# Two attention layers, experts and a recurrent cell in one pipelined kernel: the gate's weights on GpSimd, output products two a round, other orders of the instructions

## What is computed

```
layer 0: x = x + attention(norm(x), ctx)     16 heads of 8, with biases
         x = x + experts(norm(x))            gate scores over 8 experts, the best 2 count,
                                             weighted by their scores; relu between W1 and W2
layer 1: x = x + attention(norm(x), ctx)     no biases
         x = x + cell(norm(x))

cell(x): c = sigmoid(x wf + c uf + bf) * c + sigmoid(x wi + c ui + bi) * tanh(x wc + c uc)
         over the steps t; then tanh(x_t wo + c_final uo + bo) for every t
```

## Time and profile of the kernel before

| what | value |
|---|---|
| profiled execution, device time | 869.94 us |
| span from its first to its last instruction | 868.2 us |
| median of the three runs | 869.86 us |
| mean granted TensorE clock | 0.991 |
| busy: TensorE, VectorE, ScalarE, GpSimd | 836.5, 789.6, 782.3, 624.0 us |

### The profile page before, as it was taken

The page is one execution under the profiler, slowest core; times in us unless marked ns, Lnnn a source line. Parts: engine busy times, 40 slices in busy tenths (PEclk is TensorE's granted clock), DMA queues, the critical chain, the costliest instruction groups (busy, mean ns, idle before and its releaser), DMA issues. The chain is left out here.

```text
span 868.2 us, 41445 instructions
## 1 busy us (share of the span) xinstructions
PE 836.5 (96%) x15262; PEld 745.8 (86%) x15262; DVE 789.6 (91%) x2965; ACT 782.3 (90%) x2488; POOL 624.0 (72%) x1098
## 2 busy tenths in 40 slices
PE   5699999999999999999999999999999999999887
PEld 3488899999999999999999999999999999898765
DVE  4789999999999999999999999999999999999834
ACT  4699999999999999999999999999999999888754
POOL 4777887777877787777777777778777877766514
PEclk9999999999999999999999999999999999999999
DMA  9400000000000000000000000000000000000005
GB/s 337 165 3 2 3 3 4 3 4 3 3 3 3 3 3 4 3 3 4 3 4 3 3 4 3 3 4 3 4 3 3 3 3 4 3 4 2 3 2 194
DMA packets 6822, 17.68 MB, mean 20 GB/s; under 512 B 736, under 2 KB 2016, under 8 KB 6624
## 3 DMA queue, kind: packets, MB, share of 16 engines
q1 hardware_dynamic: 6336, 14.50, 4.4%
q10 hardware_dynamic: 288, 0.53, 0.2%
HBM read 10.84 MB, written 4.19 MB: 17 GB/s over the span
## 5 line engine op out<-in xcount | busy, mean ns | idle before, releaser
L1072 POOL TENSOR_TENSOR h<-Ex 128x512 f32<-128x512 f32 (+1 forms) x144 | 165.9, 1152 | 43.0 <-ACT Ex L613 42.4
L806 DVE TENSOR_REDUCE mx<-ps 128x8 f32<-128x512 f32 (+1 forms) x288 | 173.4, 623 | 14.5 <-PE ps L308 13.7
L820 DVE TENSOR_TENSOR Ex<-ps,mx 128x512 f32<-128x512 f32 (+1 forms) x288 | 172.7, 620 | 0.0
L323 PE MATMUL ps<-w,Ex 128*128 128x128 f32 x1024 | 164.0, 278 | 4.4 <-DVE Ex L820 2.9
L624 ACT ACTIVATE ET<-ps 128x512 f32<-128x512 f32 (+1 forms) x288 | 163.4, 567 | 1.2 <-PE ps L323 0.9
L613 ACT ACTIVATE Ex<-Ex 128x512 f32<-128x512 f32 (+1 forms) x288 | 164.4, 597 | 0.0
L1056 POOL TENSOR_TENSOR rs<-ve,half 128x4 f32<-128x4 f32 (+3 forms) x77 | 70.4, 914 | 128.5 <-DVE ve L796 125.8
L930 DVE SCALAR_TENSOR_TENSOR acc<-ps,we,acc 128x128 f32<-128x128 f32 x448 | 151.8, 339 | 6.0 <-PE ps L409 3.4
L662 ACT ACTIVATE hT<-ps,w 128x128 f32<-128x128 f32 x512 | 147.1, 382 | 3.4 <-PE ps L388 2.9
L388 PEld LDWEIGHTS ps<-xT,w 128*128 128x128 f32 x1024 | 124.2, 191 | 24.6 <-issue 24.6
L409 PE MATMUL ps<-w,hT 128*128 128x128 f32 x1024 | 141.8, 281 | 1.1 <-DVE Ex L820 1.0
(11 more groups left out here) (105 smaller groups left out, 1800.3 us busy)
## 6 DMA issues: line engine op xcount, KB each, us to landing
out_dram<-x SPq DMA_DIRECT2D x15, 256.0 KB, 2.7
cx<-ctx_dram SPq DMA_DIRECT2D x7, 512.0 KB, 12.7
x<-x_dram SPq DMA_DIRECT2D x7, 512.0 KB, 13.6
w<-weights_dram SPq DMA_DIRECT2D x2, 576.0 KB, 7.6
w<-weights_dram SPq DMA_DIRECT2D x1, 512.0 KB, 5.4
w<-weights_dram ACTq DMA_DIRECT2D x1, 264.0 KB, 3.7
w<-weights_dram ACTq DMA_DIRECT2D x1, 256.0 KB, 3.2
cx<-ctx_dram SPq DMA_DIRECT2D x1, 256.0 KB, 5.5
```

The costliest lines, as they stand in the source:

```text
L323: m = e.transpose(b[:, 128 * n:128 * n + 128], Ex[:, j % 2, r, 128 * n:128 * n + 128], ident)
L806: e.tensor_reduce(mx[:, j % 2, r, 4 * lo:4 * hi], b[:, 256 * lo:256 * hi].rearrange("p (j k) -> p j k", k=64), AX.X, ALU.max).then_inc(sig ...
L820: e.tensor_tensor(Ex[:, j % 2, r, 256 * lo:256 * hi].rearrange("p (j k) -> p j k", k=64), b[:, 256 * lo:256 * hi].rearrange("p (j k) -> p ...
L1072: e.tensor_tensor(u, v[:, :, :, 0:32], v[:, :, :, 32:64], ALU.add).then_inc(sig("half1"), 1)
```

## The change

1. **Gate's weights on GpSimd.** `gate_float` and `gate_weights` of VectorE are gone. GpSimd's `gate_sum` now does the conversion and the two products as well, each with a wait for the one before.
2. **Output products.** `NW` goes from 8 to 9 groups, in two uses `wx0` and `wx1` a round, from round 72 on; the first five `inputs_share` groups follow them in the same places, so all fourteen are made in rounds 72 to 78. Behind the loop come the biases, `uo` and the `cell_share` of each group. The banks of the tail are named anew (`ENDS`), since the last transposes still hold one. VectorE adds cU's part for four groups of two tiles instead of one, `TAIL` has 18 groups.
3. **First keys.** The keys of tile 0 are made in round 0 instead of 1; those of the others stay.
4. **Biases and clearing in parts.** The eight steps of `bias_pieces` run two a round in rounds 1 to 4; b2 moves from the file of W2 to that of Wq, which is loaded earlier. The clearing runs in four parts in rounds 6 to 9. `project_bias` and its sum run a round later.
5. **Orders.** All engines' lists, `LAG` and `USES` (23 uses) are new. Some parts move a round: xT is copied at lag 1 instead of 0, qT at 1 instead of 2, e0, e3 and the sums at 4 instead of 3, y1 and the first four additions at 3 instead of 2. In the new list the seventh before `pv` is S0, before `q` S1, before `yb` S2, before `wx1` S3. L1, L2, L3 stay, and so does the round of the last half step; `LAST` is one less.
6. **Warm-up.** VectorE clears `acc` at the start, and TensorE makes five products of 128 x 128 by 256 columns of these zeros before it waits for the identity.

```diff
+NW, EARLY = 9, 5
+WARM = 5
-WIDTHS = [512, 161, 528, 1024, 1152, 256, 1152]
+WIDTHS = [512, 161, 656, 1024, 1024, 256, 1152]
...
             def keys_values(i):
                 t = i - LAG["kv"]
-                if not on(t):
+                if t == 0 or not -1 <= t < NT:
                     return
                 b = bank(i, "kv")
+                t = max(t, 0)
...
+            def out_inputs(i, u):
+                g = 2 * (i - LAST_STEP + 6) + u
+                if not 0 <= g < NW + EARLY:
+                    return
+                if g >= NW:
+                    inputs_share(g - NW)
+                    return
...
+            e.wait_ge(sig("zeros"), 1)
+            for n in range(WARM):
+                e.matmul(lstm[:, 0:256], acc[:, 0, :], acc[:, :, :], start=True, stop=True)
...
+                turn_e(i, 0)
+                experts(i, 1)
                 step(i, 1)
+                turn_e(i, 3)
                 gate(i)
-                turn_e(i, 2)
                 turn_w(i)
                 turn_r(i)
-                out_inputs(i)
+                turn_e(i, 2)
                 hidden(i, 0)
-                turn_e(i, 1)
+                out_inputs(i, 0)
                 scores(i)
                 hidden(i, 1)
                 cell_inputs(i)
-                expert_bias(i)
+                turn_e(i, 1)
                 keys_values(i)
                 step(i, 0)
                 values(i)
+                query(i)
+                expert_bias(i)
+                out_inputs(i, 1)
                 experts(i, 0)
-                turn_e(i, 3)
                 turn_x(i)
-                turn_e(i, 0)
-                experts(i, 1)
                 project(i)
-                query(i)
...
+                exps(i, 1)
+                exps(i, 0)
+                out_inputs(i, 1)
+                turn_x(i)
+                widen(i)
                 turn_e(i, 0)
-                widen(i)
                 gates(i, 1)
-                query(i)
+                turn_w(i)
+                turn_e(i, 3)
+                turn_r(i)
                 turn_e(i, 2)
...
                 scale(i)
                 gates(i, 0)
                 keys_values(i)
-                exps(i, 0)
-                exps(i, 1)
-                turn_e(i, 3)
-                turn_x(i)
+                query(i)
...
-                if i == FIRST + 6:
-                    bias_pieces()
+                if FIRST + 1 <= i < FIRST + 5:
+                    bias_pieces(2 * (i - FIRST) - 2)
+                    bias_pieces(2 * (i - FIRST) - 1)
...
-                e.wait_ge(sig("wab"), t + 1)
+                e.wait_ge(sig("tix"), t + 1)
+                e.tensor_copy(tif[:, s, :], tix[:, s, 0:2]).then_inc(sig("tif"), 1)
+                e.wait_ge(sig("tif"), t + 1)
+                e.tensor_scalar(wa[:, s, :], iota, tif[:, s, 0:1], top[:, s, 0:1], ALU.is_equal, ALU.mult)
+                e.tensor_scalar(wb[:, s, :], iota, tif[:, s, 1:2], top[:, s, 1:2], ALU.is_equal,
+                                ALU.mult).then_inc(sig("wab"), 1)
...
+                gate_pieces(i)
+                spread_values(i)
+                add_bias(i)
                 keys(i, 1)
                 halves(i, 0)
-                spread_values(i)
                 spread(i)
                 gate_sum(i)
                 halves(i, 1)
                 keys(i, 0)
-                add_bias(i)
-                gate_pieces(i)
```

More of the change, by code:

```diff
@@ L112, in build @@
         identb = sb("identb", [P, 128], BF16)
-        half = sb("half", [P, 4])
         xn = sb("xn", [P, 2, 4, 128])
@@ L116, in build @@
         mv = sb("mv", [P, 2, 4, 2])
+        half = sb("half", [P, 4])
         ones = sb("ones", [P, 8])
+        nm = sb("nm", [P, 2, 4])
         ve = sb("ve", [P, 2, 4])
-        nm = sb("nm", [P, 2, 4])
         mr = sb("mr", [P, 2, 4])
@@ L185, in bank_of, with end_bank @@
             return banks[(len(USES) * (j + LAG["S" if name[0] == "S" else name]) + PLACE[name]) % 7]
+        last = bank_of("turnx", NT + L3 - 1)
+        ENDS = [b for b in banks[0:7] if b is not last] + [last, lstm]
+        def end_bank(k):
+            return ENDS[MINE.index(k) % EARLY] if k in MINE else ENDS[5 + 2 * (SIDE.index(k) % 2)]
         def sync_program(e):
@@ L433, in out_inputs, with inputs_share, cell_share @@
                                  skip_group_check=True)
-                m.then_inc(sig("wx"), 1)
+                m.then_inc(sig(f"wx{u}"), 1)
+            def inputs_share(m):
+                lo = TAIL[MINE[m]][1]
+                if m == 0:
+                    for name, reader, _, chain, step, first in USES:
+                        if name != "turnx":
+                            e.wait_ge(sig(reader), step * (SPAN[chain][1] - 1) + first)
+                if m >= EARLY:
+                    e.wait_ge(sig("out"), MINE[m - EARLY] + 1)
+                e.wait_ge(sig("xT"), lo + 4 + L3)
+                for n in range(4):
+                    e.matmul(end_bank(MINE[m])[:, 128 * n:128 * n + 128], cx[:, lo + n, :], wT[:, WX, :], start=(n == 0),
+                             stop=False, skip_group_check=True)
+            def cell_share(m):
+                e.matmul(end_bank(MINE[m])[:, :].rearrange("p (t d) -> p t d", t=4), ident,
+                         cU[:, :].unsqueeze(1).to_broadcast([P, 4, 128]), start=False, stop=True,
+                         skip_group_check=True).then_inc(sig("pre_pe"), 1)
             def cell_inputs(i):
@@ L498, in tensor_program @@
                 values(i)
+                query(i)
+                expert_bias(i)
+                out_inputs(i, 1)
                 experts(i, 0)
-                turn_e(i, 3)
                 turn_x(i)
-                turn_e(i, 0)
-                experts(i, 1)
                 project(i)
-                query(i)
-            for _, reader, _, chain, step, first in USES:
-                e.wait_ge(sig(reader), step * (SPAN[chain][1] - 1) + first)
-            for n in (6, 5):
-                e.matmul(banks[n][:, 0:128], ident, bo1, start=True, stop=False, skip_group_check=True)
-            inputs_share(0)
+            for n in (5, 6):
+                e.matmul(ENDS[n][:, 0:128], ident, bo1, start=True, stop=False, skip_group_check=True)
             e.wait_ge(sig("C"), 2 * NT + 1)
@@ L515, in tensor_program @@
                 for g in (0, 64):
-                    m = e.matmul(banks[n][g:g + 64, 0:128], c_end, wT[:, UO, :], start=False, stop=True,
+                    m = e.matmul(ENDS[n][g:g + 64, 0:128], c_end, wT[:, UO, :], start=False, stop=True,
                                  skip_group_check=True)
                 m.then_inc(sig("uo"), 1)
-            for m in range(1, 5):
-                inputs_share(m)
             e.wait_ge(sig("cU"), 1)
-            for m in range(len(mine)):
-                if m >= 5:
+            for m in range(len(MINE)):
+                if m >= EARLY:
                     inputs_share(m)
@@ L978, in vector_program @@
                 combine(i, 8)
[L979 removed]
+                stats_inputs(i)
+                update(i, 1)
                 stats_experts(i)
```

195 lines of the change are left out of this document (81 added, 114 removed), and 30 rows, old and new, of tables (LAG, USES).

## The result

The changed kernel takes 853.17 us (median of 4 runs, 852.65 to 853.61) against 868.69 us (4 runs, 866.58 to 869.94): ratio 0.9826, interval 0.9806 to 0.9847. The forecast was 851.5 us, range 845 to 861. The profiled execution took 852.91 us, its span is 851.1, against 869.94 and 868.2: 17.1 us of span.

A forecast was written before the change was run, and what follows sets the result against it. TensorE was taken to bound the full rounds, leaving gains at the two ends. Filling with start -11.5, idling up to 130 us -0.5, drain +1.0 and tail -7.4 gave -18.4 us: 851.5 us, range 845 to 861.

The forecast's parts named there:

- The tail: From the last half step to the end: 7.4 us won, with cU and the outputs coming sooner.
- the 0.3 us for a last half step at full clock: In the tail: 0.3 us more won if the last half step takes 0.54 us instead of 0.87.
- Bias pieces: In parts in rounds 1 to 4, they end TensorE's 3.68 us idling in round 5, which goes from 9.77 to 5.5 us.
- The start: Up to the first scores: they begin 1.5 us sooner, at 10.0 us instead of 11.47.
- The filling rounds: Rounds 2 to 6, up to the scores of round 7: 10 us won beyond the start's 1.5 us.
- The path to the next scores becomes that of the keys: Filling rounds: scores, key products, copy and Km set the round, 4.9 us each in rounds 2 and 3.
- the rival that I gave 0.13 for rounds 4 to 6: Half clock in the filling: each of these rounds some 1.3 us longer, 855.5 us in all; chance 0.13.
- full clock from the start: Rival: the products on zeros raise the clock, scores at 9.3 us, rounds 2 and 3 at 3.9, 849 us; chance 0.10.
- Full rounds: The 49 rounds from 130.38 to 732.84 us: no change, within 3 us either way.
- The drain: Rounds 72 to 78: 1.0 us lost to the added output groups in rounds 72 and 73, bounds 0 and 1.8.
- the rival to which I gave 0.08: Drain: each of six added groups lengthens its round by 0.9 us, 5.4 less the 1.0 counted, 856 us; chance 0.08.
- The slower case: A stall in every full round, TensorE waiting for ScalarE's late rT; with 0.45 us a round 873.5 us; chance 0.07.

The follow-up runs named there:

- shares_behind: Changed kernel with the five early output groups of rounds 76 to 78 made behind the last half step; ratio 0.9895 to the kernel before.
- before_parts: Kernel before with only the bias pieces in parts (b2 in the file of Wq) and the clearing in four parts; 861.93 us against 868.40, ratio 0.9922.
- bias_block: Changed kernel with all eight bias pieces together ahead of round 6 and the clearing in one; ratio 0.9884 to the kernel before.
- keep_clock: Changed kernel with six more products on zeros in rounds 3 to 5 and the output bias product a round later; ratio 0.9824 to the kernel before.
- no_warm: Changed kernel without the five warm-up products on zeros; ratio 0.9859 to the kernel before.
- exps_later: Changed kernel with two of ScalarE's exponentials, in rounds before 7, moved behind its later copies; ratio 0.9872 to the kernel before.
- gate_behind_step: Changed kernel with the gate's product directly behind the half step, ahead of the transposes; ratio 0.9867 to the kernel before.
- drain_moved: Changed kernel with four early groups and the nine product groups in rounds 70 to 76, a second one in 74 and 75; ratio 0.9811 to the kernel before.

## Why the prediction was right, and where it was not

**The tail** (7.4 forecast, 6.9 measured) was right step by step: cU at 3.4 us, the first cell share at 3.7, VectorE's list without a gap (9.91 us for 18 groups), DMA engines full, end at 18.7 us. One term was counted twice: the 0.3 us for a last half step at full clock was added to steps that had that half step at full clock already (they count 0.5 us of it). shares_behind shows that the groups made early carry the gain. What was not foreseen is the clock: without them it fell, in this order of the instructions, and the tail lost 1.4 us more than their own length. Likewise before_parts won 1.4 us in its tail without touching it, by its clock alone. Of the 6.9 us won, then, some 1.4 may be the clock's, an estimate from these two traces.

**Bias pieces** were the surest part of the filling: 3.7 us of idling and the half clock behind it, in both directions (bias_block +4.3 us at round 7, before_parts -5.3). Both kernels move the clearing along with the pieces, so what it gives by itself is not shown. The parts ran cheaply in rounds 1 and 2 (both subtractions 0.289 us). The last two, in round 4, met Km. The instructions of VectorE's line 961 in the changed kernel (shortest, median and longest in ns, starts in us), and then GpSimd's timeline at that place:

```profile
L961 DVE SCALAR_TENSOR_TENSOR b2s<-b2p,w,b2s x2: 339/664/990, 17.9 to 18.3; 72x128 bf16<-72x128 bf16 x2
```

```profile
18.15 1.04 POOL L1033 TENSOR_TENSOR Km<-kT,w 128x512 f32<-128x512 f32 x1 [0.78 <-ACT kT L560]
```

The second began at 18.3 us, inside Km (18.15 to 19.19), and took 0.990 us against 0.339. The Trainium skill's rule (SBUF — State Buffer, "SBUF: two separate sides") named this case, and I had checked it for the subtractions alone. It cost nearly nothing here: the reciprocal was done at 19.95 us, and ScalarE, which stands before the next step with rd, was itself busy until 19.94. In keep_clock, where ScalarE was free sooner, the same pieces made it wait 0.74 us.

**The start** (1.5 forecast, 1.9 measured) came out by two parts: some 1.1 us by the keys in round 0, as no_warm shows, and some 0.8 by the warm-up, which the sum did not count.

**The filling rounds** (10.0 forecast, 5.3 measured) are where a step failed: "The path to the next scores becomes that of the keys", 4.9 us in rounds 2 and 3. Round 2 took 4.57, but round 3 7.26, round 4 7.13 instead of 5.4, round 5 5.92 instead of 5.5, round 6 7.04 instead of 6.5. Rounds 5 and 6, where the bias pieces had stood, won 4.9 of the 5.8 us forecast; rounds 2 to 4, which were to win 4.2 by the new orders, won 0.5 (18.96 us against 19.44). Two things were missing in it. First, from round 3 on the way from kT to the next scores leads through ScalarE's whole list. This is that list in round 5 of the changed kernel, at full clock:

```profile
30.69 0.37 ACT L560 ACTIVATE kT<-ps,w 128x128 f32<-128x128 f32 x1
...
31.79 0.36 ACT L620 ACTIVATE qT<-ps,w 128x128 f32<-128x128 f32 x1
32.03 0.72 ACT L632 ACTIVATE Ex<-Ex 128x256 f32<-128x256 f32 x2
32.65 0.38 ACT L589 ACTIVATE xT<-ps 128x256 f32<-128x256 f32 x1
32.91 0.31 ACT L655 ACTIVATE rd<-ri 128x128 f32<-128x128 f32 x1
33.11 0.66 ACT L643 ACTIVATE ET<-ps 128x256 f32<-128x256 f32 x2
33.73 0.28 ACT L668 ACTIVATE rT<-ps 128x128 f32<-128x128 f32 x1
33.95 0.38 ACT L643 ACTIVATE ET<-ps 128x256 f32<-128x256 f32 x1
```

3.6 us without a gap between kT and the copy for which the scores wait; with scores, e1, keys and the scaling ahead of it that is the 5.92 us of this round. Behind the key products I had counted the copy kT and GpSimd's Km alone. That this list is the path is read from the traces; exps_later, which shortened it, let another loop close and so does not prove it. Second, the clock: it fell in rounds 3 and 4, the rival that I gave 0.13 for rounds 4 to 6; keep_clock puts its price at about 2 us. And its counterpart, full clock from the start (0.10), came true until 14.4 us. Both rivals happened, one after the other.

**Full rounds** (0 forecast, 4.1 won). The step was "an error of 0.06 us a round, about half of one such switch, times 49 is the 3 us": the size was 0.084. I counted only how many runs of small tiles there are, and not what stands behind them: the gate's product gains 0.10 us when transposes precede it, and the transposes lose 0.03. gate_behind_step gives 3.6 of the 4.1 us back. The remaining 0.01 us a round is not pursued.

**The gate's weights**, the first part of the change, are worth nothing measurable. VectorE was off the bound, as argued; GpSimd paid 1.25 us a round between mr and the sum, where I had 0.6 to 0.9; TensorE had no wait by it in full rounds, and 0.50 us in round 6.

**The drain** (1.0 lost forecast, 2.3 measured, and 3.3 against before_parts, whose drain has no half clock). It lies beyond the bounds, 0 to 1.8. From half step to half step, rounds 72 to 76 are 1.2, 1.0, 0.7, 0.3 and 0.4 us longer than in before_parts; drain_moved, without the second group in rounds 72 and 73, has them 1.1 and 0.7 us shorter again, and rounds 70, 71 and 74 longer by 1.0, 0.7 and 0.4. So it went in the direction of the rival to which I gave 0.08, at a price below its 4.4.

**The slower case** did not come: TensorE is idle for 0.01 us in 49 full rounds.

## What to carry to other kernels

Cut the run into stages by events that both traces have, and look in each for what the bound engine does: here a change that names VectorE, GpSimd and the output won its time with a few idle microseconds of TensorE at both ends, and with the order of its own products. Within a bound engine, see what stands ahead of each short product: here the gate's, behind transposes instead of small tiles, was worth 0.07 us a round. Move each part of a change alone before giving it a share: of six parts here, one, tried alone on the kernel before, won as much from round 2 to round 7 as all six together. Follow each engine's whole list from the event to its reader, not only the data path: in filling rounds the list is the path, and moving two instructions to the end of one list lengthened the loop through another engine's.

## What the runs showed of the hardware

- Five products on zeros from 1.17 us on: the clock rises at 4.2 to 7.3 us in eleven traces with them, at 22.6 to 29.4 in three without. In the changed kernel it fell again at 14.4 us; in the 3.4 us before, TensorE was busy for 1.36, with no wait longer than 1.48.
- Work that fills TensorE's gaps can pay through the clock as well: without the output groups of rounds 76 to 78 it fell for 10.2 us just ahead of the tail. In before_parts, in the old order and also without them, it did not.
- A GpSimd TENSOR_SCALAR on 128x8 with two scalar operands from SBUF takes 0.40 us, a TENSOR_TENSOR of that size 0.20.
- A VectorE SCALAR_TENSOR_TENSOR with two inputs in SBUF that starts inside GpSimd's Km takes 0.99 us instead of 0.34.
- The gate's two matmuls of 128x128 weights and 8 columns take 0.24 us together behind the half step's 128*32 tiles and 0.14 behind transposes.
